# Sorting the first expert layer's tokens for half of the batches

## The chip, the cores and the metric

The kernel runs on one core of a Trainium2 chip, as one launch. The metric is the device time of that launch in microseconds (us). TensorE (PE), VectorE (DVE), ScalarE (ACT), GpSimd (POOL) and the DMA queue of SyncE (SP) run their own programs and meet through semaphores.

## What is computed

Two layers over x, 4 batches of 512 tokens with 256 features. Cut to what matters:

```python
# layer 0, for each batch b
w_bot = einsum('g,got->ot', cond_8[b], weight * mask)      # a projection mixed from 8
h = x @ w_bot.T + bias
probs = softmax(h @ router_w.T);  top 2 of 8 experts, weights topk_w
x = x + sum over the 2 chosen experts e of topk_w[e] * (h @ W0[e] + probs[e])    # W0[e]: 256x256
# layer 1, for each batch b
h = x @ W_base.T + b_base + lora(cond_8[b])
shared = 2 experts for all tokens: (silu(h @ wg) * (h @ wu)) @ wd                # hidden width 352
routed = the same form, for the top 2 of 8 other experts of each token
x = x + shared + routed
```

All products are made of f16 halves: a value is split in a high and a low part, and three products (high by high, low by high, high by low) are summed.

## The kernel before

A **tile** is 128 tokens; there are 16, four to a batch. Three stages follow each other.

**Dense layer 0** (main PE loop over `m` in `range(TWO)`, TWO = 8, two tiles a step). For each of the 16 tiles TensorE multiplies by all 8 experts: for each pair of experts `j` 6 matmuls of 512 columns into one PSUM bank (`group`, L1000). VectorE adds `coef * result` to `x1` for every expert, chosen or not (L777, 8 a tile; `coef` is 0 for the six not chosen). Four banks turn, so TensorE is at most two pairs ahead of VectorE. Laid between: `transposes(m)` turns the finished tiles of `x1`, ScalarE and VectorE split them (`tr_hi`, `tr_lo`), `layer1_input(c)` projects batch c for layer 1, `h_hi`/`h_lo` split the result, `logits(1, c)` gives its gate values, `token_rows` and `copy_rows` turn it into rows of tokens, which SP stores in HBM (`keep`, `token_store`).

At the same time the 21,760 columns of layer 1 weights are loaded and split in 16 **pieces** of 1,360 columns, through two buffers. SP may load piece n when piece n-2 is through (`s_pclo` at n-1 or more). ScalarE makes the high half and scales the piece (`split_piece`, L529 and L532), GpSimd subtracts in eight parts (L442) to give the low half. ScalarE takes two pieces in each step m, at places fixed in its program.

**Shared steps.** The shared experts' work is 24 steps, six to a batch (`ST`). A step is `gate_up(i)` on TensorE (12 matmuls of 512 columns, the sixth of a batch 6), a silu on ScalarE (L572), a product on VectorE (`prod`, L904), a copy to f16 on ScalarE (`acts`, L582) and a subtraction on VectorE (L910). After six, `down(c)` (68 matmuls of 256 columns) and four `accumulate` follow. The first EARLY = 18 steps run before the routed loop. Among them the chosen experts of all 2,048 tokens become slots of a sorted list: `largest`, `second` (13 small VectorE instructions), `ranks` on TensorE, `groups`, `slots`, `hot_lanes`, `hot_tiles`, `inverse` on TensorE, `slot_tokens`, `tile_experts`, one of them after each of steps 2 to 14.

**Routed loop and end.** 39 tiles of 128 slots, each of one expert. GpSimd fetches rows by index (L451) and puts results by index (L456). After it SP loads the results, ScalarE scales them, GpSimd adds one (L470), VectorE the other (`combine`, L892), beside the last six shared steps.

## Time and profile before

| | us |
|---|---|
| median of 3 runs (lowest, highest) | 379.43 (377.74, 380.24) |
| the profiled execution, its own time | 378.77 |
| its span, first to last instruction | 377.0 |
| TensorE busy in the span | 357.7 |
| VectorE, ScalarE, GpSimd busy | 238.8, 166.1, 154.2 |
| mean granted TensorE clock | 0.994 of full |

The page gives for each engine the busy time, for each line of code a group of instructions with its mean length, and the idle time before it with the instruction that ended the idle time. The timeline gives the same in order of time. A program of this kind has no scheduler: each engine does its own list in the written order, and an instruction that waits holds up all that stands behind it on its engine.

### The profile page before, as it was taken

How to read it: one execution, taken by the hardware profiler on the slowest of the kernel's cores; microseconds unless marked ns; L12 is line 12 of the kernel's file. 1: busy time of each engine (PE TensorE's matmuls, PEld its weight loads, DVE VectorE, ACT ScalarE, POOL GpSimd, SP SyncE). 2: the span in 40 equal slices, each digit the busy share in tenths (PEclk: the TensorE clock that was granted, in tenths of full speed). 3: DMA queues.
4: the chain of work that ended last, by engine and by line, in shares of the span. 5: the costliest groups of instructions: out<-in, count | busy, mean ns of one | idle time of the engine just before them, and what ended most of it. 6: DMA issues, size and time to landing. Idle time of an engine off the chain costs nothing.

```text
span 377.0 us, 7974 instructions
## 1 busy us (share of the span) xinstructions
PE 357.7 (95%) x2713; PEld 225.4 (60%) x2714; DVE 238.8 (63%) x594; ACT 166.1 (44%) x286; POOL 154.2 (41%) x241
## 2 busy tenths in 40 slices
PE   7998999999999999989999999999999999999992
PEld 3543544455454454555447677777777777776561
DVE  1357999676766646778775455565555565546476
ACT  1045376567555765543442333333333333323560
POOL 3000564665647532000020365565665555532642
PEclk9999999999999999999999999999999999999997
DMA  7985113433443420100000122222222222212942
GB/s 217 377 330 203 54 53 119 150 92 122 141 151 128 136 69 0 58 0 2 0 28 2 44 86 84 70 84 78 75 83 80 73 78 78 80 42 74 353 161 111
DMA packets 18038, 39.26 MB, mean 104 GB/s; under 512 B 2976, under 2 KB 9376, under 8 KB 17888
## 3 DMA queue, kind: packets, MB, share of 16 engines
q1 hardware_dynamic: 13552, 28.71, 22.8%
q0 software_dynamic: 3744, 10.23, 8.7%
q8 instruction: 14, 0.23, 0.3%
q10 hardware_dynamic: 720, 0.02, 0.1%
q14 instruction: 8, 0.07, 0.1%
HBM read 29.65 MB, written 9.31 MB: 103 GB/s over the span
## 4 chain that ended last, share of the span: by engine, by line
PE 72%; DVE 16%; DMA 4%; ACT 3%; issue 3%; SPq 0%; DVEq 0%
PE bank L1000 58%; PE bank L1147 4%; PE bank L1245 3%; DVE prod L904 2%; PE bank L1016 2%; PE bank L1229 2%; ACT acts L582 2%; DVE x L892 2%; DMA w1s<-results 2%; DVE x L777 2%; DVE acts L910 1%; DMA x<-wc 1%; PE bank L1076 1%; DMA results<-yb,row_out 1%; ACT sil L572 1%
## 5 line engine op out<-in xcount | busy, mean ns | idle before, releaser
L442 POOL TENSOR_TENSOR w1s<-piece,w1s 128x170 f16<-128x170 f32 x128 | 61.6, 521 | 78.2 <-ACT piece L532 78.2
L1000 PE MATMUL bank<-w0s,hs 128*128 128x512 f16 x384 | 86.0, 379 | 1.2 <-DVE x L777 1.2
L1000 PE MATMUL bank<-w1s,rT 128*128 x468 | 76.2, 313 | 1.6 <-DVE rT L964 1.6
L451 POOL DMA_INDIRECT rows<-token_store,row_in x39 | 37.9, 971 | 86.1 <-DVE row_in L874 47.5
L777 DVE SCALAR_TENSOR_TENSOR x<-bank,coef,x 128x256 f32<-128x256 f32 x128 | 54.8, 478 | 19.4 <-PE bank L1000 19.1
L1000 PEld LDWEIGHTS bank<-w0s,hs 128*128 128x128 f16 x384 | 36.9, 98 | 43.8 <-DVE x L777 1.9
L1000 PE MATMUL bank<-hs,w1s 128*128 128x512 f16 x264 | 59.6, 379 | 2.1 <-DVE prod L904 2.1
L1000 PEld LDWEIGHTS bank<-w1s,rT 128*128 128x128 f16 x468 | 44.0, 98 | 22.1 <-issue 2.1
L456 POOL DMA_INDIRECT results<-yb,row_out x39 | 38.5, 987 | 37.1 <-ACT yb L606 37.1
L1000 PE MATMUL bank<-w1s,aT 128*128 (+1 forms) x351 | 44.8, 273 | 0.8 <-DVE aT L957 0.8
L600 ACT ACTIVATE ract<-prod 128x352 f16<-128x352 f32 x39 | 19.4, 497 | 58.5 <-DVE prod L970 33.6
L1000 PEld LDWEIGHTS bank<-hs,w1s 128*128 128x128 f16 x264 | 25.0, 98 | 32.3 <-DVE prod L904 5.2
L964 DVE COPY rT<-bank 128x256 f32<-128x256 f32 x39 | 16.6, 425 | 33.3 <-PE bank L1229 33.3
L1000 PEld LDWEIGHTS bank<-w1s,aT 128*128 128x128 f16 (+1 forms) x351 | 32.7, 98 | 4.5 <-issue 0.9
L973 DVE TENSOR_TENSOR ract<-prod,ract 128x352 f16<-128x352 f32 x39 | 20.5, 526 | 21.9 <-issue 18.5
L1147 PE MATMUL bank<-w1s,acts 128*128 128x256 f16 x272 | 30.5, 273 | 1.5 <-DVE slot_lo L839 1.2
L595 ACT ACTIVATE sil<-bank 128x352 f32<-128x352 f32 x39 | 18.1, 463 | 28.5 <-PE bank L1000 28.5
L1147 PEld LDWEIGHTS bank<-w1s,acts 128*128 128x128 f16 x272 | 26.4, 98 | 6.1 <-issue 1.7
L582 ACT ACTIVATE acts<-prod 128x512 f16<-128x512 f32 (+1 forms) x24 | 15.1, 629 | 30.7 <-DVE prod L904 30.7
L529 ACT ACTIVATE w1s<-piece 128x1360 f16<-128x1360 f32 x16 | 21.3, 1329 | 14.7 <-DMA piece<-w 14.7
L910 DVE TENSOR_TENSOR acts<-prod,acts 128x512 f16<-128x512 f32 (+1 forms) x24 | 16.7, 697 | 16.0 <-ACT acts L582 16.0
L532 ACT ACTIVATE piece<-piece 128x1360 f32<-128x1360 f32 x16 | 21.4, 1338 | 0.5
(149 smaller groups left out, 405.5 us busy)
## 6 DMA issues: line engine op xcount, KB each, us to landing
piece<-w SPq DMA_DIRECT2D x16, 680.0 KB, 3.9
w1s<-results SPq DMA_DIRECT2D x6, 512.0 KB, 8.3
x<-wc SPq DMA_DIRECT2D x4, 512.0 KB, 7.0
w1s<-xT SPq DMA_DIRECT2D x4, 512.0 KB, 11.0
w1s<-w SPq DMA_DIRECT2D x4, 512.0 KB, 10.1
token_store<-xrow SPq DMA_DIRECT2D x4, 512.0 KB, 3.3
out<-x SPq DMA_DIRECT2D x8, 256.0 KB, 2.2
x<-x SPq DMA_DIRECT2D x1, 1536.0 KB, 11.7
```

What stands on the lines that cost most here:

```text
L442: ins = nc.gpsimd.tensor_tensor(w1s[:, LO, at], piece[:, i % 2, part], w1s[:, HI, at], ALU.subtract)
L451: pool.indirect_dma_start(rows[:, i % 2], None, token_store, bass.IndirectOffsetOnAxis(row_in[:, i:i + 1], 0)).then_inc(s_row[i % 2], 16)
L456: pool.indirect_dma_start(results, bass.IndirectOffsetOnAxis(row_out[:, i:i + 1], 0), yb[:, i % 2], None).then_inc(s_put[i % 2], 16)
L529: nc.scalar.activation(w1s[:, HI, i * PIECE:(i + 1) * PIECE], piece[:, i % 2], ACT.Copy, scale=SW).then_inc(sm["s_pchi"], 1)
L532: nc.scalar.activation(piece[:, i % 2], piece[:, i % 2], ACT.Copy, scale=SW).then_inc(sm["s_pcsc"], 1)
L582: nc.scalar.activation(acts[0:M, c % 2, f, HI], prod[0:M, p], ACT.Copy).then_inc(sm["s_ahi"], 1)
L600: nc.scalar.activation(ract[:, q, HI], prod[:, q, 0:F], ACT.Copy).then_inc(sm["s_rhi"], 1)
L777: nc.vector.scalar_tensor_tensor(x1[:, t], bank[(n + a) % 4][:, h * D:(h + 1) * D], coef[:, t, e:e + 1], x1[:, t], ALU.mult, ALU.add).then ...
L910: nc.vector.tensor_tensor(low, prod[0:M, p], acts[0:M, c % 2, f, HI], ALU.subtract).then_inc(sm["s_alo"], 1)
L973: nc.vector.tensor_tensor(ract[:, q, LO], prod[:, q, 0:F], ract[:, q, HI], ALU.subtract).then_inc(sm["s_rlo"], 1)
L1000: mm = nc.tensor.matmul(out_ap, l, r, start=(i == 0), stop=(i == len(terms) - 1))
L1147: mm = nc.tensor.matmul(bank[4 + q][:, 0:D], acts[:, c % 2, f, a, q * P:(q + 1) * P], w_dn(b, f), start=(f == 0 and n == 0), stop=(f == ST ...
```

## The change

Batches 0 and 1 (tiles 0 to 7) keep the dense layer 0. Batches 2 and 3 (tiles 8 to 15) get a sorted one: TensorE turns their layer 0 input into rows (`rows_of_layer0`), VectorE works out a slot for each of the 2,048 choices (`slots0`), GpSimd scatters the rows into `slot_rows` in HBM (16 indirect DMAs), SP loads 23 tiles of slots, TensorE turns each (`operand_rows`) and multiplies it by one expert (`sorted_tile`, 6 matmuls of 256 columns), SP stores the results in `slot_out`, GpSimd gathers them (16 indirect DMAs) and VectorE adds them with their weights (`combine0`, four instructions for two tiles). The sorted tiles run in bursts of four behind the shared steps 2 to 7. The dense loop has 4 steps m instead of 8. EARLY is 21 instead of 18; the dense stage's work for batches 2 and 3 and `down(0)`, `down(1)` stand behind step 11, the ranks and slots of layer 1 behind steps 12 to 19. Pieces are taken in the order 0 to 9, 13, 14, 15, 10, 11, 12, and pieces from the ninth on are split among the shared steps, since the first layer's weights and buffers now lie where they go.

The core of the diff:

```diff
-    EARLY = 3 * ST
-    DOWN = {ST + 1: 0, EARLY - 1: 1, EARLY + 1: 2}
+    EARLY = 3 * ST + 3
+    DOWN = {EARLY + 1: 2}
...
+    TILES0 = (NTR * P * K_TOP + E * (P - 1)) // P
+    BURST = 4
+    BURST_AT = 2
+    DEEP = 4
...
+    ORDER = [*range(FREE), *range(KEPT, NP), *range(FREE, KEPT)]
...
+            for n in range(FREE - 2):
+                load_piece(n)
...
+            keep(0)
+            sp.wait_ge(sm["s_placed"], 16 * K_TOP * NTR)
+            for i in range(DEEP):
+                load_rows0(i)
+            load_piece(FREE - 2)
+            for i in range(TILES0):
+                if i + DEEP < TILES0:
+                    load_rows0(i + DEEP)
+                keep_out0(i)
+                if i == BURST:
+                    load_piece(FREE - 1)
...
+            for n in range(4):
+                low_parts(n)
+            pool.wait_ge(sm["s_slots0"], 1)
+            pool.wait_ge(sm["s_zero"], 16 * 2)
+            for t in range(NTR):
+                for k in range(K_TOP):
+                    place(t, k)
+            for n in range(4, FREE):
+                low_parts(n)
+            for b in range(DEEP):
+                pool.wait_ge(s_kept0[b], 16 * len(range(b, TILES0, DEEP)))
+            for t in range(TPB):
+                take(t)
+            low_parts(FREE)
+            for t in range(TPB, NTR):
+                take(t)
...
+                if m == 1:
+                    copy_rows0(range(NTD, NTD + TPB))
...
+                if i == 10:
+                    exps(2, DENSE, 1.0 / (SH1 * SW))
+                if i == 11:
+                    tr_hi(4)
+                    piece_hi(FREE + 2)
+                    tr_hi(5)
+                    piece_scaled(FREE + 2)
+                    h_hi(1, 2)
+                    tr_hi(6)
+                    tr_hi(7)
+                    h_hi(1, 3)
...
+                if i == 11:
+                    transposes(4)
+                    down(0, quarters=(0, 1))
+                    transposes(5)
+                    down(0, quarters=(2, 3))
+                    layer1_input(2)
+                    transposes(6)
+                    down(1, quarters=(0, 1))
+                    transposes(7)
+                    down(1, quarters=(2, 3))
+                    layer1_input(3)
```

**GpSimd.** From the first subtraction on, before:

```order
L442 TENSOR_TENSOR w1s<-piece,w1s 128x170 x128
L451 DMA rows<-token_store,row_in 128x512 x6
L456 DMA results<-yb,row_out 4352x256
```

and now:

```order
L545 TENSOR_TENSOR w1s<-piece,w1s 128x170 x32
L555 DMA slot_rows<-xrow,idx 2944x512 x16
L545 TENSOR_TENSOR w1s<-piece,w1s 128x170 x48
L560 DMA yg<-slot_out,idx 128x256 x8
L545 TENSOR_TENSOR w1s<-piece,w1s 128x170 x8
L560 DMA w1s<-slot_out,idx 128x256 x8
L545 TENSOR_TENSOR w1s<-piece,w1s 128x170 x40
L590 DMA rows<-token_store,row_in 128x512 x6
```

The subtractions of the fifth piece now stand behind 16 scatters, which wait for the slot numbers (`s_slots0`).

**ScalarE** in step m = 3 of the dense loop, with the rows of the change (the rows before are the same up to their line numbers, with two additions of the bias instead of four): the halves of layer 1's input (L618), the seventh piece (L672, L677), the turned tiles (L658), the LoRA weights, the bias, the token rows (L663), the eighth piece.

```order
L618 ACTIVATE hs<-bank,b_sc 128x512 [waits s_h,s_bsc]
L618 ACTIVATE hs<-bank,b_sc 128x512 [waits s_h]
L672 ACTIVATE w1s<-piece 128x1360 [waits s_piece6]
L677 ACTIVATE piece<-piece 128x1360 [waits s_pchi]
L658 ACTIVATE xrow<-bank 128x2x256 [waits s_tr]
L697 ACTIVATE wls<-wl 128x512 [waits s_wlf]
L654 ACTIVATE x<-x,st 128x256 x4
L663 ACTIVATE xrow<-bank 128x512 [waits s_rt] x4
L672 ACTIVATE w1s<-piece 128x1360 [waits s_piece7]
L677 ACTIVATE piece<-piece 128x1360 [waits s_pchi]
```

The order is kept; what the wait for `s_piece6` hangs on has moved.

**ScalarE** from shared step 10 to the first turned tiles of batch 2, now (no such stretch before):

```order
L738 ACTIVATE sil<-bank 128x512 [waits s_prod,s_gu]
L750 ACTIVATE acts<-prod 128x512 [waits s_prod]
L672 ACTIVATE w1s<-piece 128x1360 [waits s_m0,s_piece11]
L640 ACT_TABLE_LOAD
L640 ACTIVATE ex<-ex 128x64 [waits s_exq]
L738 ACT_TABLE_LOAD [waits s_prod]
L738 ACTIVATE sil<-bank 64x512 [waits s_gu]
L750 ACTIVATE acts<-prod 64x512 [waits s_prod]
L677 ACTIVATE piece<-piece 128x1360 [waits s_pchi]
L658 ACTIVATE xrow<-bank 128x2x256 [waits s_tr]
```

The exponentials of the first two batches, with their two table loads, stand between steps 10 and 11.

## Rows read from the trace of the kernel before

**Rows 1.** The page, part 1: busy us, share of span, instructions.

```profile
PE 357.7 (95%) x2713; PEld 225.4 (60%) x2714; DVE 238.8 (63%) x594; ACT 166.1 (44%) x286; POOL 154.2 (41%) x241
```

**Rows 2.** Windows: stretch, its length, busy us of each engine, granted clock, DMA.

```profile
136.66:206.62 69.96, 65.97 (x461) 38.01 (x458) 47.76 (x130) 32.57 (x51) 5.88 (x10) 1.00 0.06 20
85.30:136.66 51.36, 51.36 (x316) 25.97 (x314) 33.46 (x75) 32.12 (x39) 30.12 (x64) 1.00 0.39 123
```

**Rows 3.** Timeline of TensorE: start us, us, line, what.

```profile
81.21 0.61 PE L1087 MATMUL bank<-ident,hs 128*128 128x128 f16 x8
81.66 2.75 PE L1000 MATMUL bank<-w0s,hs 128*128 128x512 f16 x12
...
85.30 5.34 PE L1000 MATMUL bank<-w0s,hs 128*128 128x512 f16 x24
```

**Rows 4.** Groups by line and shape: count, busy us, mean ns, idle before.

```profile
L1000 PE MATMUL bank<-w0s,hs 128*128 128x512 f16 x384 | 86.0, 379 | 1.2 <-DVE x L777 1.2
L442 POOL TENSOR_TENSOR w1s<-piece,w1s 128x170 f16<-128x170 f32 x128 | 61.6, 521 | 78.2 <-ACT piece L532 78.2
L1147 PE MATMUL bank<-w1s,acts 128*128 128x256 f16 x272 | 30.5, 273 | 1.5 <-DVE slot_lo L839 1.2 <-DVE acts L910 0.3
L532 ACT ACTIVATE piece<-piece 128x1360 f32<-128x1360 f32 x16 | 21.4, 1338 | 0.5
L964 DVE COPY rT<-bank 128x256 f32<-128x256 f32 x39 | 16.6, 425 | 33.3 <-PE bank L1229 33.3
L524 ACT ACTIVATE xrow<-bank 128x512 f16<-128x512 f16 x16 | 8.7, 595 | 11.0 <-PE bank L1087 11.0
```

**Rows 5.** Timeline of VectorE in the dense stage.

```profile
46.64 0.25 DVE L721 COPY lg<-bank 128x96 f32<-128x96 f32 x1
...
50.59 3.23 DVE L777 SCALAR_TENSOR_TENSOR x<-bank,coef,x 128x256 f32<-128x256 f32 x8
...
65.31 0.68 DVE L749 SCALAR_TENSOR_TENSOR wl<-wb_in,bank 128x512 f32<-128x512 f32 x1
```

**Rows 6.** Timeline of GpSimd: its two indirect DMAs with no wait between.

```profile
191.63 1.16 POOL L451 DMA_INDIRECT rows<-token_store,row_in  x1 [47.48 <-DVE row_in L874]
193.10 0.95 POOL L451 DMA_INDIRECT rows<-token_store,row_in  x1 [0.30 <-issue]
```

**Rows 7.** The page, part 6: DMA issues, KB each, us to landing.

```profile
piece<-w SPq DMA_DIRECT2D x16, 680.0 KB, 3.9
out<-x SPq DMA_DIRECT2D x8, 256.0 KB, 2.2
```

**Rows 8.** Timeline of VectorE among the shared steps.

```profile
168.79 1.39 DVE L848 TENSOR_SCALAR yg<-lane,slot_lo 128x128 f16<-128x128 f16 x8
...
175.76 0.69 DVE L904 SCALAR_TENSOR_TENSOR prod<-bank,sil 128x512 f32<-128x512 f32 x1 [0.35 <-ACT sil L572]
177.15 0.69 DVE L910 TENSOR_TENSOR acts<-prod,acts 128x512 f16<-128x512 f32 x1 [0.70 <-ACT acts L582]
177.76 1.45 DVE L854 TENSOR_TENSOR wls<-tile,slot_hi 128x1248 f16<-128x1248 f16 x1
```

**Rows 9.** Timeline of ScalarE: a table load before the exponentials.

```profile
168.17 1.28 ACT L501 ACT_TABLE_LOAD   x1
```

**Rows 10.** Timeline of VectorE: the first routed tile, and the end.

```profile
206.62 0.41 DVE L964 COPY rT<-bank 128x256 f32<-128x256 f32 x1
...
367.16 5.02 DVE L892 SCALAR_TENSOR_TENSOR x<-w1s,st,x 128x256 f32<-128x256 f32 x8
372.21 1.42 DVE L922 SCALAR_TENSOR_TENSOR x<-bank,x 128x256 f32<-128x256 f32 x4
```

**Rows 11.** Windows of 1 us at the end, columns as in Rows 2.

```profile
369.00:370.00 1.00, 0.54 (x5) 0.23 (x3) 1.00 (x2) 0.00 (x0) 1.00 (x2) 1.00 0.22 86
...
372.00:373.00 1.00, 0.00 (x0) 0.00 (x0) 0.97 (x4) 0.00 (x0) 0.00 (x0) 0.62 0.21 76
373.00:374.00 1.00, 0.00 (x0) 0.00 (x0) 0.63 (x2) 0.00 (x0) 0.00 (x0) 0.50 0.18 70
```

More of the change, by code:

```diff
@@ L899, in shared_dve @@
                 up = bank[2 * p + 1][0:M] if f < ST - 1 else bank[2 * p][0:M]
+                last = len(turned_rows(i)) - 2
+                first = max(last - 2, 0)
+                for t in turned_rows(i)[:first]:
+                    operand0(t)
                 dve.wait_ge(sm["s_sil"], i + 1)
@@ L906, in shared_dve @@
                 if i == 1:
-                    h_lo(1, B - 1)
+                    h_lo(1, 1)
+                for t in turned_rows(i)[first:last]:
+                    operand0(t)
                 dve.wait_ge(sm["s_ahi"], i + 1)
@@ L928, in _ @@
+            tr_lo(TWO_D - 1)
             for i in range(EARLY):
                 shared_dve(i)
[L930 to L940 removed]
@@ L941, in _ @@
-                if i == 12:
+                if i == 9:
+                    dve.wait_ge(sm["s_m0"], TILES0)
+                    take_logits(1, 0, DENSE)
+                    largest(DENSE)
+                    second(DENSE)
+                    selected(DENSE, "s_sel")
+                if i == 11:
+                    combine0(8)
+                    tr_lo(4)
+                    accumulate(0, (), (0, 1))
+                    combine0(10)
+                    tr_lo(5)
+                    accumulate(0, (), (2, 3))
+                    h_lo(1, 2)
+                    combine0(12)
+                    tr_lo(6)
+                    accumulate(1, (), (0, 1))
+                    combine0(14)
+                    tr_lo(7)
+                    accumulate(1, (), (2, 3))
+                    h_lo(1, 3)
@@ new lines, in _ @@
+                if i == 12:
+                    take_logits(1, 1, SORTED)
+                    largest(SORTED)
+                    second(SORTED)
+                    selected(SORTED, "s_sel")
+                if i == 14:
+                    dve.wait_ge(sm["s_rank"], 1)
+                    groups(rank1[:, NT * E:])
+                    slots()
+                if i in (15, 16):
+                    hot_lanes(2 * (i - 15))
+                    hot_lanes(2 * (i - 15) + 1)
+                if i == 17:
+                    for n in range(3):
+                        hot_tiles(n)
@@ new lines, in sorted_tile, with experts0 @@
+            def sorted_tile(i, expert_at):
+                pe.wait_ge(sm["s_x0"], i + 1)
+                if i >= 2:
+                    pe.wait_ge(sm["s_y0"], i - 1)
+                group(bank[6 + i % 2][:, D:2 * D],
+                      [(rT0[:, i % 2, a, k], w1s[:, b, bass.ds(expert_at + (W0 + k * E * D), D)])
+                       for k in range(KT) for a, b in PASSES], "s_m0")
+            def experts0(ap):
+                return nc.values_load_multi_w_load_instructions(
+                    ap, engines=(nc.tensor.engine,), min_val=0, max_val=(E - 1) * D,
+                    skip_runtime_bounds_check_because="the table's entries are clamped where it is made")[1]
```

548 lines of the change are left out of this document (380 added, 168 removed).

## The prediction

> **What bounds the kernel now.** I read the page's busy times first: TensorE is busy 357.7 of 377.0 us [rows 1]. Then the windows of the two stretches that the change rebuilds: in 85.30 to 136.66 (steps m = 4 to 7 of the dense loop) it is busy all of 51.36 us, in 136.66 to 206.62 (from `gate_up(0)` to the first routed tile) 65.97 of 69.96 [rows 2]. So TensorE sets the pace and 12.1 us of saved TensorE work (below) could be a gain. But VectorE is busy 47.8 of the second stretch's 70 us, and its timeline shows why that is nearly all it can do: of each shared step it works 0.69, waits 0.70 for ScalarE's copy, and works 0.69 [rows 8]. The slack is thin, and every engine runs a fixed list.
>
> **TensorE's work before the routed loop.** Removed: 8 tiles x 24 dense matmuls = 192, at 86.0 / 384 = 0.224 us: 43.0 [rows 4]. Added: 23 sorted tiles x 6 = 138 matmuls of 256 columns at 30.5 / 272 = 0.112: 15.5; 92 + 32 transposes, 8 in the 0.45 between two starts: 0.056 each, 7.0 [rows 3]; the small ranks 0.6; three shared steps that come forward from behind the loop 7.8 (12 matmuls each). Net -12.1. The rest is moved. From here the question is who is late. I follow the written order with row durations; times are on the clock of the trace before.
>
> **Step 1, to `gate_up(0)`.** Until m = 1 nothing changes but a cast: VectorE begins m = 1 at 50.8 instead of 50.59 [rows 5]. In m = 1 TensorE stands before the rows of tile 10 until ScalarE has copied tile 8, which ScalarE does behind `tr_hi(0)` and `wl_hi(1)`: 56.2 instead of 51.9. The rows of tiles 14 and 15 wait once more, behind the bias, which needs `shares0`. VectorE is 4.0 late at m = 2. The ranks on TensorE hold it again, `groups` cost 1.4 and `slots0` 1.3, so that it passes the point where it stood at 65.31 [rows 5] at 74.8, and the slot numbers are there.
>
> GpSimd then issues 16 scatters. The only pair without a wait gives 0.95 + 0.30 = 1.25 a scatter [rows 6]; the busy part alone, 0.95, is the lower bound, the pair's start to start, 1.47, the upper. I take 1.27 with a little for the wait each carries: 20.3, ending at 95.1. Behind them the fifth piece's subtraction takes 8 x 61.6 / 128 = 3.85 [rows 4]. Only then may SP load the seventh piece, which needs its buffer: 3.9 to landing [rows 7]. It is there at 102.9, where ScalarE has waited since 84.7. Behind the wait stand its two passes of 1.34 each [rows 4], the turned tiles, LoRA weights, four additions of the bias, and the four copies of token rows for which TensorE stands since 93.3. It resumes at 108.9, and `gate_up(0)` starts at **109.5** instead of 136.66: -27.2. Without the scatters in the way it would be 93.9. The hold of 15.6 is the largest single wait.
>
> **Step 2, `gate_up(0)` to the end of the sorted tiles.** Steps 0 and 1, `layer1_input(1)` and step 2 reach the burst after 11 us. A burst is 4 x (0.67 + 0.22) = 3.6 of TensorE work with 2.6 of gate_up. VectorE (four copies of 0.425 [rows 4], 2.1 for the step) and ScalarE (four copies, a silu, a copy, one pass of a piece: 4.0) fit. What does not quite fit is the load of the last tile of a burst: SP may issue it only when the first result of the burst is stored, and a load takes about 2.2 [rows 7]: 0.5 a burst. The tenth piece's load stands in the same queue: 2.0 once. Sum 48.7 for 43.9 of work. `gate_up(0)` + 48.7 is S.
>
> **Step 3, steps 8 to 11.** TensorE has 10.0 of work. GpSimd gathers once the last result is stored (S + 3.2); the first four gathers land by S + 10.3. They are not the last to come: ScalarE has in steps 8 to 11 four pairs of silu and copy, four token rows (8.7 / 16 = 0.54 each [rows 4]), four passes of a piece (5.4), and the exponentials with two table loads of 1.28 [rows 9]; VectorE puts 15 small instructions of batches 0 and 1 in between (3.3, by 3.95 for the 96-column form, 46.64 to 50.59 [rows 5]). Followed in order: step 11's subtraction ends at S + 20.8, four `combine0` of 0.63 [rows 10] at S + 23.3. TensorE idles 13.4.
>
> **Step 4, the block behind step 11.** TensorE 22.2: 136 matmuls x 0.112, 4 transposes of tiles, two `layer1_input`. Three times it then waits for VectorE's accumulate and the next combine0: 2.9 + 3.9 + 2.9. Ends S + 54.7.
>
> **Step 5, steps 12 to 20.** TensorE 27.7. VectorE has the other batches' top two (3.3), `groups` and `slots` (3.8), 32 hot lanes (1.39 for 8 [rows 8]: 5.6), `hot_tiles` 3.5, `slot_tokens` 1.6 and `tile_experts` 1.8 beside nine steps of 2.1; before they had steps 2 to 14 to lie in, now 12 to 19. ScalarE has 4.4 a step in steps 12 to 15 and again two table loads. In order: hot tiles ready at S + 90.9, row numbers at S + 94.4, expert numbers at S + 99.1, `gate_up(20)` ends S + 102.6; the first routed copy follows step 20's subtraction at S + 105.3. That is `gate_up(0)` + 154.0 where before it was 69.96 [rows 2]: **+84.0**. The first routed copy is at 263.5 instead of 206.62 [rows 10].
>
> **Step 6, the end.** The routed loop is the same. Behind it three shared steps are gone: VectorE lost 2.1 to each between combines, up to 372.21 [rows 10]. Its other work stays, and GpSimd's 16 additions cap what it gains: **-5.5**.
>
> **The clock.** [...] How long it stays there no row of the trace shows: the lower bound is 0; for the upper I let down's first two quarters (3.8) and `gate_up(0)` and half of (1) (3.9) take double. I take the middle, 1.9 each: **+3.8**. [...]
>
> **Sum.** 378.77 (the profiled execution, span 377.0) - 27.2 + 84.0 - 5.5 + 3.8 = 433.9. The median of the three runs is 0.7 above that execution, within their spread of 2.5. **Forecast 434.**
>
> **Rivals.**
> - *TensorE stays the bound* (faster). If no engine is ever later than TensorE, the gain is 12.1 + 5.5: 361. For it: rows 1. Against it: it needs all the waits above (some 65 us) to vanish; it decides from the point where the seventh piece is there before TensorE is through m = 3, at 93.3 by my chain, 9.6 before it can be. 3%.
> - *Only the scatters' hold counts*: from `gate_up(0)` on, TensorE's 103.8 of work runs without waits: 378.77 - 27.2 + 33.8 - 5.5 = 380. The change does not do what it should, nor harm. 4%.
> - *Half of the late waits*: order costs less than I chain, steps 3 to 5 overlap in part: about 405. 13%.
> - *GpSimd's indirect DMAs cost more back to back* than the one pair shows, 2.5 us each as their 128 KB are written: +20 on step 1 and something on step 3, 456. 9%.
> - *The clock stays low* in the sparse stretch from S: 50 us of TensorE work, half of it on the path, doubled: +25, 459. 8%.
> - Forecast, its own range 421 to 443 (scatters 15.2 to 23.5 in all, step 2 45 to 50, clock 0 to 7.7): 63%.
>
> The range for 8 in 10 is 402 to 450. Within 1% counts as no change. Faster 3%, same 3%, slower 94%.
>
> **What would show it.** Right: 16 scatters in a row on GpSimd that end near 95 and an idle time of ScalarE before the seventh piece of about 18 us, ended by its load; `gate_up(0)` near 109; TensorE idle before the turning of tile 8, ended by combine0; VectorE over 90% busy in steps 14 to 18; the first routed tile near 263. Wrong: scatters under 0.8 us, or a first routed tile before 235, which would mean that the orders of steps 8 to 20 overlap better than written.

## The result and the profile after

| | before | after |
|---|---|---|
| median (lowest to highest), us | 379.36 (377.74 to 380.24), 4 runs | 460.21 (459.58 to 462.46), 4 runs |
| the profiled execution, its span | 378.77, 377.0 | 462.46, 460.7 |
| mean granted TensorE clock | 0.994 | 0.901 |

The change is slower, with a ratio of 1.2148 (95% interval 1.2089 to 1.2207). The forecast was 434 and the range 402 to 450: the direction and most of the mechanism held, the size did not. Some 26 us more were lost than I had summed.

The page, part 1, after, which answers to [rows 1]: busy us, share of the span, instructions.

```profile
PE 363.9 (79%) x2799; PEld 234.7 (51%) x2800; DVE 244.4 (53%) x605; ACT 181.2 (39%) x320; POOL 190.3 (41%) x274
```

Over the whole span TensorE has some 20 us less to multiply (the prediction's 12.1 ahead of the loop, and the 7.8 of the three steps that only moved), but is busy for 6 us more than before. So it took some 26 us longer for its work (an estimate: 363.9 against 357.7 less 19.9): part of it ran at a lower granted clock, 0.901 of full in the mean against 0.994. Windows of the changed kernel: stretch, its length, busy us of PE, weight load, DVE, ACT, POOL, then the granted clock, DMA share and GB/s.

```profile
60.00:75.00 15.00, 12.34 (x70) 5.89 (x69) 9.01 (x27) 8.08 (x10) 2.59 (x6) 0.81 0.10 42
100.00:120.00 20.00, 5.74 (x22) 3.13 (x23) 4.40 (x11) 11.05 (x16) 13.32 (x28) 0.50 0.40 126
185.00:200.00 15.00, 0.23 (x1) 0.23 (x2) 9.12 (x14) 7.12 (x8) 12.55 (x17) 0.62 0.53 175
200.00:215.00 15.00, 12.90 (x77) 9.98 (x77) 4.24 (x9) 3.64 (x4) 7.14 (x16) 0.70 0.20 62
260.00:275.00 15.00, 8.68 (x48) 4.15 (x49) 12.16 (x31) 6.51 (x9) 7.85 (x11) 0.62 0.00 1
```

Before, the clock was 1.00 in the stretches of [rows 2]. Now it is 0.50 to 0.81 in these stretches, in which TensorE has stood, and still low when the work starts again: 0.50 in 114 to 120, 0.58 in 199 to 207, 0.50 in 261.7 to 267.

GpSimd, after, timeline (start us, us, line, what, and in brackets the idle time before and what ended it): the first and the last of the sixteen scatters, and the fifth and sixth pieces' subtractions behind them.

```profile
80.18 1.17 POOL L555 DMA_INDIRECT slot_rows<-xrow,idx  x1 [3.99 <-DVE idx L999]
...
99.76 0.96 POOL L555 DMA_INDIRECT slot_rows<-xrow,idx  x1 [0.30 <-issue]
100.74 7.46 POOL L545 TENSOR_TENSOR w1s<-piece,w1s 128x170 f16<-128x170 f32 x16
```

ScalarE, after: the seventh piece's first pass.

```profile
108.42 1.34 ACT L672 ACTIVATE w1s<-piece 128x1360 f16<-128x1360 f32 x1 [18.84 <-DMA piece<-w]
```

The sixteen take 20.6 us, 1.285 each: the pair of [rows 6] had the right price. ScalarE stands 18.84 us before the seventh piece, as forecast (about 18). TensorE, after, timeline: the same hold as it sees it, then the later waits and the work behind them.

```profile
56.54 1.01 PE L1375 MATMUL bank<-ident,hs 128*128 128x128 f16 x8 [4.37 <-ACT xrow L686]
57.35 5.21 PE L1284 MATMUL bank<-w1s,hs 128*128 128x512 f16 x12
...
114.26 1.09 PE L1400 MATMUL bank<-ident,hs 128*128 128x128 f16 x8 [16.16 <-ACT xrow L663]
115.14 2.77 PE L1284 MATMUL bank<-hs,w1s 128*128 128x512 f16 x6
...
144.13 0.55 PE L1501 MATMUL bank<-ident,w1s 128*128 128x128 f16 x4 [3.03 <-DMA w1s<-slot_rows]
144.53 4.27 PE L1284 MATMUL bank<-hs,w1s 128*128 128x512 f16 x12
...
166.47 2.75 PE L1284 MATMUL bank<-hs,w1s 128*128 128x512 f16 x12 [0.56 <-issue]
...
199.77 1.12 PE L1363 MATMUL bank<-ident,x 128*128 128x128 f32 x4 [16.54 <-DVE x L1035]
200.68 6.32 PE L1468 MATMUL bank<-w1s,acts 128*128 128x256 f16 x34
...
220.83 0.66 PE L1363 MATMUL bank<-ident,x 128*128 128x128 f32 x4 [3.14 <-DVE x L1035]
...
261.77 5.30 PE L1284 MATMUL bank<-hs,w1s 128*128 128x512 f16 x12 [5.59 <-DVE prod L1113]
271.62 2.26 PE L1524 MATMUL bank<-wls,yg 128*128 128x78 f16 x32 [4.55 <-DVE wls L1064]
...
283.42 4.80 PE L1284 MATMUL bank<-hs,w1s 128*128 128x512 f16 x12 [5.17 <-DVE te L1090]
291.43 3.41 PE L1284 MATMUL bank<-w1s,rT 128*128 x12 [2.99 <-DVE rT L1248]
```

Twelve matmuls of 512 columns take 2.75 us at the full clock (at 166.47) and 5.2 to 5.3 here behind a wait of 4.4 or 5.6 (granted 0.56 in 57 to 63, 0.50 in 261.7 to 267); a routed tile's first twelve take 3.41 where before they took 1.96. The stretches against my forecast:

| from to | forecast, us | measured, us | miss |
|---|---|---|---|
| start to `gate_up(0)` | 109.5 | 115.1 | +5.6 |
| to `gate_up(8)` (S) | 48.7 | 58.0 | +9.3 |
| to the turning of tile 8 | 23.3 | 26.7 | +3.4 |
| to `gate_up(12)` | 31.4 | 34.3 | +2.9 |
| to the first routed tile's products (50.6 to its copy, 0.6 on) | 51.2 | 57.3 | +6.1 |
| to the last instruction (169.8 before, less 5.5) | 164.3 | 169.3 | +5.0 |
| clock, a term of its own | 3.8 | in the rows above | -3.8 |

Together +28.5, and the span is 28.6 longer than 377.0 + 55.1. This execution is the slowest of its four; the median stands 2.3 us under it. With the same code up to there, `gate_up(0)` starts at 113.2 to 114.9 in the profiles of experiments 4, 6, 8, 10 and 11, and the row "to `gate_up(12)`" takes 31.3 to 32.2 in experiments 4, 8, 10 and 11. So a difference of 2 or 3 us between two profiles is no effect by itself.

### The profile page after: what moved, and what is told of

The parts are those of the page before. It is cut to its first block, busy times and chain, and to the rows that moved or that the text cites. A ratio compares the mean times of both kernels' runs of the same rounds, so it can differ in the third digit from the quotient of the medians.

```text
span 460.7 us, 8449 instructions
## 1 busy us (share of the span) xinstructions
PE 363.9 (79%) x2799; PEld 234.7 (51%) x2800; DVE 244.4 (53%) x605; ACT 181.2 (39%) x320; POOL 190.3 (41%) x274
## 4 chain that ended last, share of the span: by engine, by line
PE 55%; DVE 17%; DMA 9%; ACT 8%; issue 5%; POOL 4%; SPq 1%; DVEq 0%; ACTq 0%
PE bank L1284 42%; PE bank L1468 4%; POOL slot_rows L555 3%; DMA w1s<-slot_rows 3%; PE bank L1608 3%; PE bank L1592 2%; DVE x L1097 2%; DMA piece<-w 2%; DVE prod L1113 2%; DMA w1s<-results 2%; DVE x L1035 1%; DMA x<-wc 1%; ACT acts L750 1%; DVE x L1156 1%; PE bank L1300 1%
## 5 line engine op out<-in xcount | busy, mean ns | idle before, releaser
L545 POOL TENSOR_TENSOR w1s<-piece,w1s 128x170 f16<-128x170 f32 x128 | 64.9, 543 | 147.7 <-ACT piece L677 147.7
L1284 PE MATMUL bank<-w1s,rT 128*128 x606 | 96.6, 307 | 6.2 <-DVE rT L1248 3.9
L1284 PE MATMUL bank<-hs,w1s 128*128 128x512 f16 x264 | 70.9, 425 | 13.8 <-DVE prod L1113 7.5
L1284 PEld LDWEIGHTS bank<-w1s,rT 128*128 128x128 f16 x606 | 56.8, 99 | 31.2 <-issue 7.8
L1284 PE MATMUL bank<-w1s,hs 128*128 128x512 f16 x192 | 49.2, 416 | 0.0
L1113 DVE SCALAR_TENSOR_TENSOR prod<-bank,sil 128x512 f32<-128x512 f32 (+1 forms) x24 | 16.5, 688 | 42.1 <-ACT sil L738 42.0
L1468 PE MATMUL bank<-w1s,acts 128*128 128x256 f16 x272 | 34.3, 292 | 0.0
L1156 DVE SCALAR_TENSOR_TENSOR x<-bank,coef,x 128x256 f32<-128x256 f32 x64 | 26.7, 474 | 13.0 <-PE bank L1284 12.9
L1284 PEld LDWEIGHTS bank<-w1s,hs 128*128 128x128 f16 x192 | 19.7, 105 | 24.7 <-issue 7.2
L1468 PEld LDWEIGHTS bank<-w1s,acts 128*128 128x128 f16 x272 | 28.6, 105 | 5.3
L672 ACT ACTIVATE w1s<-piece 128x1360 f16<-128x1360 f32 x16 | 21.3, 1329 | 23.9 <-DMA piece<-w 23.9
L790 ACT ACTIVATE sil<-bank 128x352 f32<-128x352 f32 x39 | 18.1, 463 | 25.1 <-PE bank L1284 25.1
L738 ACT ACTIVATE sil<-bank 128x512 f32<-128x512 f32 (+1 forms) x24 | 14.3, 595 | 34.0 <-PE bank L1284 33.8
## 6 DMA issues: line engine op xcount, KB each, us to landing
w_raw<-w SPq DMA_DIRECT2D x4, 512.0 KB, 11.1
```

Source lines behind the costliest of these rows:

```text
L545: ins = nc.gpsimd.tensor_tensor(w1s[:, LO, at], piece[:, n % 2, part], w1s[:, HI, at], ALU.subtract)
L672: nc.scalar.activation(w1s[:, HI, ORDER[n] * PIECE:(ORDER[n] + 1) * PIECE], piece[:, n % 2], ACT.Copy, scale=SW).then_inc(sm["s_pchi"], 1)
L790: nc.scalar.activation(sil[:, q, 0:F], bank[2 * q][:, 0:F], ACT.Silu, scale=1.0 / (SH1 * SW)).then_inc(sm["s_rsil"], 1)
L1113: nc.vector.scalar_tensor_tensor(prod[0:M, p], up, SA / (SH1 * SW), sil[0:M, p], ALU.mult, ALU.mult).then_inc(sm["s_prod"], 1)
L1156: nc.vector.scalar_tensor_tensor(x1[:, t], bank[(n + a) % 4][:, h * D:(h + 1) * D], coef[:, t, e:e + 1], x1[:, t], ALU.mult, ALU.add).then ...
L1284: mm = nc.tensor.matmul(out_ap, l, r, start=(i == 0), stop=(i == len(terms) - 1))
```

## The experiments

The times are medians of four runs (twelve in the fifth), against 460.21 for the change and some 379.5 for the kernel before.

**1. Subtractions among the scatters.**

```diff
-            for n in range(4):
+            for n in range(5):
                 low_parts(n)
...
             for t in range(NTR):
+                if t == 4:
+                    low_parts(5)
                 for k in range(K_TOP):
                     place(t, k)
-            for n in range(4, FREE):
+            for n in range(6, FREE):
```

> The change, but GpSimd subtracts the fifth piece ahead of the sixteen scatters and the sixth after eight of them. Theory (the scatters hold the seventh piece, and through it ScalarE's list and TensorE): the fifth piece was scaled at 76.1, so its 3.8 end at 80, when the slot numbers come; the seventh piece lands near 84, ScalarE's idle time of 18.8 before it goes, gate_up(0) starts near 99 instead of 115.1, the whole is about 16 us shorter: 444. Rival 1 (something else would hold TensorE there, for instance the loads of the sorted tiles behind the last scatter at 104.4): under 5 us of it remain. Rival 2 (scatters are slow for their writes, and slow the subtractions beside them): subtractions over 5 us a piece, scatters over 1.5 each, gain under 8.

447.55 us, ratio 1.1762 (1.1721 to 1.1803): 12.7 less than the change. The hold is gone, and something new stands in its place. GpSimd, experiment 1:

```profile
91.82 3.78 POOL L545 TENSOR_TENSOR w1s<-piece,w1s 128x170 f16<-128x170 f32 x8
...
105.72 7.92 POOL L545 TENSOR_TENSOR w1s<-piece,w1s 128x170 f16<-128x170 f32 x16
```

VectorE, experiment 1:

```profile
106.46 6.83 DVE L1123 TENSOR_TENSOR acts<-prod,acts 128x512 f16<-128x512 f32 x1 [0.70 <-ACT acts L752]
```

TensorE, experiment 1:

```profile
98.99 1.46 PE L1286 MATMUL bank<-hs,w1s 128*128 128x512 f16 x6
115.27 0.81 PE L1286 MATMUL bank<-rs,hs 128*128 128x8 f16 x24 [5.31 <-DVE hs L832]
```

`gate_up(0)` starts at 98.99 (expected near 99). But VectorE's subtraction of 0.69 us [rows 8] lasts 6.83: it began behind the start of a row of sixteen subtractions on GpSimd and ended 0.35 before that row did. TensorE waits 5.31 for what stands behind it. From `gate_up(0)` to these 24 small matmuls it is 16.3 us instead of 13.4, so 2.9 of the 16.2 gained went there; against the 10.8 that this stretch takes in experiment 2, at the full clock and without the hold by GpSimd, it is 5.5. Neither theory had it.

**2. Unused matmuls (spins) in the two long waits.**

```diff
+            def spin(n, b, col):
+                for _ in range(n):
+                    nc.tensor.matmul(bank[b][:, D - 192:D], ident16[:], hs[:, HI, 0, col:col + 192],
+                                     start=True, stop=True)
...
                             logits(1, 0)
+                            spin(170, 7, 3 * S)
                             token_rows(0, (2, 3))
...
                 if i == 11:
+                    pe.wait_ge(sm["s_x0"], TILES0)
+                    pe.wait_ge(sm["s_rows"], ND * TPB)
+                    spin(170, 5, 0)
                     transposes(4)
```

> The change, with 170 unused matmuls of 192 columns (some 14 us) on TensorE in each of its two longest waits (16.2 us before the token rows of tiles 2 and 3, 16.5 before the turning of tile 8); their results are read by nothing. It prices the clock alone. [...] Rival (what is slow is VectorE's and ScalarE's chain, and TensorE at half clock is hidden beside it): the granted clock is full in 100 to 120 and 186 to 215, but the time moves by under 2 us. If the matmuls outlast the waits, their excess shows as lost time, at most 2 us a wait.

456.43 us, ratio 1.2041 (1.1996 to 1.2086): 3.8 less, about half of the 6 to 8 that I had expected for the theory that the slow restarts lie on the path. TensorE, experiment 2:

```profile
177.87 14.19 PE L1420 MATMUL bank<-hs,ident 128*128 128x192 f16 x170
194.07 0.66 PE L1363 MATMUL bank<-ident,x 128*128 128x128 f32 x4 [2.01 <-DVE x L1035]
194.56 3.88 PE L1474 MATMUL bank<-w1s,acts 128*128 128x256 f16 x34
```

The 34 matmuls take 3.88 instead of 6.32, with the clock granted at 1.00 in 194 to 199, where the change has 0.58 in 199 to 207: the low clock was what made them slow. From `gate_up(0)` to `gate_up(8)` the profile shows 55.0 instead of 58.0, and the turnings of tiles 8 and 10 are 6.5 apart instead of 9.3. (This execution is the fastest of its four, 452.80 of up to 459.01.) Part is given back later, where the clock falls in a wait of 3.15 that left it high in the change: the third turning takes 1.12 instead of 0.66, the 34 matmuls behind it 4.94 instead of 3.88 (granted 0.74 in 210.6 to 216.5, against 1.00 in 220.8 to 225.3 of the change).

**3. Three shared steps more ahead of the loop, in the kernel before.**

```diff
-    EARLY = 3 * ST
-    DOWN = {ST + 1: 0, EARLY - 1: 1, EARLY + 1: 2}
+    EARLY = 3 * ST + 3
+    DOWN = {ST + 1: 0, 3 * ST - 1: 1, EARLY + 1: 2}
```

(and the scaling and the bank side placed as in the change)

> The kernel before, with 21 shared steps ahead of the routed loop instead of 18, and nothing else. My prediction's terms for it: 7.8 us of gate_up more ahead of the loop, 5.5 less behind it: +2.3 us, 382. Theory now (behind the loop the end hangs on the loads of the results and GpSimd's additions, and loses nothing when three steps leave): +7 us, 386 to 387, with the stretch from the loop's end to the last instruction as long as before within 1 us.

386.18 us, ratio 1.0147 (1.0108 to 1.0185): the total is the theory's, its reason is not. TensorE, experiment 3, the first routed tile:

```profile
218.21 3.70 PE L1000 MATMUL bank<-w1s,rT 128*128 x12 [2.99 <-DVE rT L964]
```

It starts 11.0 later than the 207.17 of before, not 7.8: with no `down` behind the last shared step, TensorE stands 2.99 for the first copy and then needs 3.70 for what took 1.96. The end does get shorter. The last store of a routed tile, GpSimd, experiment 3, and the same one after the change:

```profile
356.25 0.97 POOL L456 DMA_INDIRECT results<-yb,row_out  x1 [1.38 <-ACT yb L606]
```

```profile
428.37 0.97 POOL L595 DMA_INDIRECT results<-yb,row_out  x1 [1.32 <-ACT yb L801]
```

From there to the end of the span it is 28.7 here, 32.3 after the change, and 34.3 before (342.68 to 377.0). So my 5.5 for the tail was right (5.6). What hid it in the change is the closing: SP's waits at the end, first after the change, then in experiment 3 (line, what it waited for, us in total, times, longest).

```profile
SPq L106 <- PEq L106: 4.5, 1, 4.5
```

```profile
SPq L85 <- PEq L85: 1.1, 1, 1.1
```

Behind the last landing the change waits 3.4 us longer for TensorE's sequencer.

**4. The tenth piece's load ahead of the sorted tiles.**

```diff
             load_piece(FREE - 2)
+            load_piece(FREE - 1)
             for i in range(TILES0):
...
                 keep_out0(i)
-                if i == BURST:
-                    load_piece(FREE - 1)
```

> The change, with the tenth piece's load issued ahead of the loads and stores of the sorted tiles instead of after the fifth. Theory (TensorE's wait of 3.0 us at 144 for the rows of a sorted tile is for a load that stands behind the 680 KB of that piece, and the clock falls after it): the wait goes, the next 12 matmuls take 2.8 instead of 4.3, 3 to 5 us shorter, 456. Rival (the wait is of the store or load chain itself, four deep): nothing moves, 460. Rival 2: the piece collides with the rows of tiles 4 to 7 instead, and the wait moves to 133: 459 to 460.

454.28 us. Its four runs, 448.33, 452.61, 455.95 and 458.10, lie too far apart for an interval: the total says only that it is shorter, by 2 to 12 us. The size comes from the profile: from `gate_up(0)` to `gate_up(8)` it is 53.1 instead of 58.0. TensorE, experiment 4, where the wait of 3.03 and the slow twelve stood:

```profile
138.82 0.40 PE L1500 MATMUL bank<-ident,w1s 128*128 128x128 f16 x4
139.22 2.75 PE L1283 MATMUL bank<-hs,w1s 128*128 128x512 f16 x12
```

No wait, and 2.75 instead of 4.27 (granted 1.00 in 139 to 142, against 0.65 in 144.5 to 149 of the change). One load in a queue cost 3.0 us of wait and here 1.5 of clock (in experiment 2, after 2.83 in the same place, the twelve took 2.75).

**5. Twenty-nine semaphores more, in the kernel before.**

```diff
+        spare_sems = [sem(f"s_spare{c}") for c in range(29)]
```

> The kernel before with 29 more semaphores declared, as many as the change declares, and used by nothing. In the change SP's last wait, for TensorE's sequencer behind the last store, is 4.5 us; in the kernel before with 21 early steps it is 1.1. Theory (the semaphores are set back at the end, one after another): +3 to 3.5 us, 383. Rival (the closing hangs on the program's length or on the sorted stage's registers): no change, 379.6.

379.39 us, ratio 0.9998 (0.9975 to 1.0022), SP's last wait 1.1 as before. The theory falls, for semaphores that nothing uses. Every kernel built on the change shows 3.7 to 4.5 there, both built on the kernel before 1.1. The cause stays open.

**6. One top two, exponentials behind step 20.**

```diff
                 if i == 9:
                     dve.wait_ge(sm["s_m0"], TILES0)
                     take_logits(1, 0, DENSE)
-                    largest(DENSE)
-                    second(DENSE)
-                    selected(DENSE, "s_sel")
...
                     take_logits(1, 1, SORTED)
-                    largest(SORTED)
-                    second(SORTED)
-                    selected(SORTED, "s_sel")
+                    largest(ALL)
+                    second(ALL)
+                    selected(ALL, "s_sel")
...
-                if i == 10:
-                    exps(2, DENSE, 1.0 / (SH1 * SW))
-                if i == 15:
-                    exps(3, SORTED, 1.0 / (SH1 * SW))
+            exps(2, ALL, 1.0 / (SH1 * SW))
```

> The change, with the top two of all sixteen tiles of layer 1 worked out once, behind step 12, instead of twice (behind steps 9 and 12), and its exponentials once, behind step 20, instead of behind steps 10 and 15 between the silus. VectorE has 3.3 us and a wait of 3.4 beside GpSimd's subtraction less before tile 8 is turned, ScalarE two table loads there (2.6) and two in step 15. Theory (VectorE's and ScalarE's lists hold TensorE in steps 8 to 11 and 12 to 20): the turning of tile 8 comes 3 to 6 us sooner, the first routed tile 5 to 8 sooner, 453. Rival (the gathers hold it: their last for tiles 8 and 9 lands near 188, and GpSimd's list is unchanged): under 2 us. Rival 2: VectorE's list behind step 12 only gets longer by the wider forms: 459 to 460.

459.19 us, ratio 1.2088 (1.2028 to 1.2148): within 1% of the change. TensorE and VectorE, experiment 6:

```profile
191.73 1.11 PE L1357 MATMUL bank<-ident,x 128*128 128x128 f32 x4 [11.14 <-DVE x L1032]
202.69 0.66 PE L1357 MATMUL bank<-ident,x 128*128 128x128 f32 x4 [4.28 <-DVE x L1032]
...
214.46 1.11 PE L1357 MATMUL bank<-ident,x 128*128 128x128 f32 x4 [3.15 <-DVE x L1032]
215.36 6.33 PE L1462 MATMUL bank<-w1s,acts 128*128 128x256 f16 x34
```

```profile
199.51 3.12 DVE L1032 SCALAR_TENSOR_TENSOR x<-yg,part,x 128x256 f32<-128x256 f32 x4
```

The wait before tile 8 falls from 16.5 to 11.1, so the first theory was right there. Then combine0 meets GpSimd's next subtraction (3.12 for four instead of 1.66) and the wait before tile 10 rises from 2.1 to 4.3; the turnings of tiles 8 to 14 span 32.1 instead of 27.5. The larger part of that loss is the clock and not VectorE: it fell in the wait of 3.15 before tile 12 (0.59 in 214.4 to 221.7), though the change kept it high through the 3.14 at 220.83 (1.00 in 220.8 to 225.3), and the 34 matmuls behind tiles 12 and 14 take 6.33 and 5.11 instead of 3.88 each. What was saved ahead was lost behind, and a good part of it by a clock that differs between executions; the total of 459 to 460 that rival 2 named has another reason than the one it gave, since from `gate_up(12)` to the first routed tile it is 57.0, no longer than the 57.3 of the change.

**7. All of these at once, and all gathers ahead of the eleventh piece.** The edits of 1, 4 and 6, a third subtraction among the scatters (`if t == 6: low_parts(6)`), and

```diff
-            for t in range(TPB):
-                take(t)
-            low_parts(FREE)
-            for t in range(TPB, NTR):
+            for t in range(NTR):
                 take(t)
```

> Everything together that removes a wait from the change: subtractions of the fifth to seventh piece among the scatters, the tenth piece's load before the sorted tiles, one top two and one set of exponentials, all gathers ahead of the eleventh piece's subtraction. Theory (the losses are separate places of one chain): the gains add, 12.7 + 5.9 + about 7, and the 6.8 us that VectorE's subtraction waited beside GpSimd's run of sixteen in the first experiment come on top: 425 to 432. Rival (one wait replaces another): over 440. Neither expects it under the kernel before.

444.18 us, ratio 1.1695 (1.1638 to 1.1751): the rival. TensorE, experiment 7:

```profile
120.48 0.61 PE L1495 MATMUL bank<-ident,w1s 128*128 128x128 f16 x4 [5.01 <-DMA w1s<-slot_rows]
```

ScalarE, experiment 7:

```profile
173.33 1.34 ACT L672 ACTIVATE w1s<-piece 128x1360 f16<-128x1360 f32 x1 [3.67 <-DMA piece<-w]
...
189.03 1.34 ACT L672 ACTIVATE w1s<-piece 128x1360 f16<-128x1360 f32 x1 [8.15 <-DMA piece<-w]
```

The ninth and tenth pieces, 680 KB each, are now issued together at 111.6 just ahead of the rows of the fifth sorted tile, and that tile waits 5.01. With the gathers first, the pieces behind them come late, and ScalarE stands 3.67 and 8.15 us for them. These two cost TensorE nothing that the rows show: tile 8 is turned 21.0 us behind `gate_up(8)` (21.3 in experiment 6), tile 10 waits 4.28 in both, and its copy on ScalarE comes 0.03 after the turning. The block behind step 11 is long, 40.5 us to `gate_up(12)` as in experiment 6 (34.3 in the change), since its four groups of 34 matmuls run slow: 5.74, 5.54, 6.32 and 5.10.

**8. Unused matmuls in the four late waits** (50 before `gate_up(18)`, 40 before `inverse`, 45 before `gate_up(20)`, 25 before the first routed tile).

> The change, with unused matmuls of 192 columns on TensorE in the four waits before the routed tiles: 50 before gate_up(18), 40 before inverse, 45 before gate_up(20), 25 before the first routed tile (4.1, 3.3, 3.7 and 2.1 us). It prices the clock in 255 to 295. Theory (TensorE's bursts of 5.30, 2.26, 4.57, 4.80 and 3.41 us at about half clock lie on the path between VectorE's parts): 5 to 9 us shorter, 453. Rival (VectorE's list is what takes the time, TensorE only answers to it): the groups take 2.8, 1.4, 2.8, 2.8 and 2.0 us, but the first routed tile comes under 2 us sooner.

454.84 us, ratio 1.2003 (1.1952 to 1.2054): 5.4 less. TensorE, experiment 8:

```profile
256.48 2.76 PE L1284 MATMUL bank<-hs,w1s 128*128 128x512 f16 x12 [1.13 <-DVE prod L1113]
...
268.39 4.68 PE L1284 MATMUL bank<-hs,w1s 128*128 128x512 f16 x12
...
284.21 1.96 PE L1284 MATMUL bank<-w1s,rT 128*128 x12 [0.93 <-DVE rT L1248]
```

From `gate_up(17)` (249.41; 254.71 in the change) to the first routed tile it is 34.8 instead of 36.7, and that tile's twelve are 1.4 shorter: the profile gives 3.4 to the spins, between the two theories; the first routed tile alone, 1.9 sooner, fits the rival. The rest of the 5.4 lies ahead of them, where this execution restarted faster than the profiled one of the change (the turnings of tiles 8 and 10 are 8.0 apart instead of 9.3) with the same code. The spin before `inverse` was too short: 3.79 us of wait are left behind it and the next twelve still take 4.68.

**9. Mended with the collisions avoided, and spins.** Of experiment 7 without the change of the gathers, the ninth piece's load moved ahead of the wait for the scatters and the tenth's behind the first four sorted tiles' rows, with the spins of experiment 8 and 110 before tile 8.

```diff
+            load_piece(FREE - 2)
             sp.wait_ge(sm["s_placed"], 16 * K_TOP * NTR)
             for i in range(DEEP):
                 load_rows0(i)
-            load_piece(FREE - 2)
+            load_piece(FREE - 1)
```

> The subtractions of pieces five to seven among the scatters, the ninth piece's load ahead of the wait for the scatters and the tenth's behind the rows of the first four sorted tiles, one top two and one set of exponentials, the gathers in the order of the change, and unused matmuls in the waits before tile 8 (110 of 192 columns) and in the four waits before the routed tiles. Theory (the change's loss is a sum of replaceable waits and of slow restarts): what the seventh experiment lost to two pieces that met the rows of the sorted tiles (5.0 and a slow burst) and to the late twelfth piece (8.2) comes back, and the clock gives 5 more: 426 to 432. Rival (what is mended here opens the next wait): 438 or more. Both stay above the kernel before.

430.11 us, ratio 1.1344 (1.1295 to 1.1393): the theory's time, 30.1 us below the change. TensorE, experiment 9, the first sorted tile's rows, and before tile 8:

```profile
112.65 1.02 PE L1503 MATMUL bank<-ident,w1s 128*128 128x128 f16 x8 [2.63 <-DMA w1s<-slot_rows]
...
163.78 7.84 PE L1417 MATMUL bank<-hs,ident 128*128 128x192 f16 x93
173.25 0.65 PE L1360 MATMUL bank<-ident,x 128*128 128x128 f32 x4 [1.64 <-DVE x L1035]
173.74 3.87 PE L1470 MATMUL bank<-w1s,acts 128*128 128x256 f16 x34
```

The first line of the spins is where the view begins; all 110 take 9.24 from 162.38. Against experiment 7 the profile is 19.0 shorter, in two places mainly: 54.0 instead of 60.4 from `gate_up(0)` to `gate_up(8)`, where the collision went, and 29.8 instead of 40.5 from the turning of tile 8 to `gate_up(12)`, where all four groups of 34 take 3.87 or 3.88 (7.2 less) and tile 10 waits 2.10 instead of 4.28. So the clock gave more than the 5 expected, and the late twelfth piece not the 8.2. After the wait of 2.63 above the clock was low too, 0.59 in 112.65 to 115.1: eight transposes took 1.02 instead of 0.61.

**10. The expert taken as number 0 for all sorted tiles** (`places0 = [0] * BURST`), so TensorE loads no register in a burst. The kernel leaves out the choice of the first layer's expert.

> The change with the first layer's expert taken as number 0 for all 23 sorted tiles instead of read from the table, so that TensorE loads no register in a burst (its result is left out of the computation; matmuls, loads and stores are the same). Theory (six groups of register loads stall TensorE 0.4 to 0.6 us each behind steps 2 to 7, not in my sum): 2 to 3 us shorter there, 457.5. Rival (TensorE has slack for them beside the loads of the rows): under 1 us. SP's last wait of 4.5 us: if it hangs on these loads it falls to 1.1.

457.03 us, ratio 1.2067 (1.2007 to 1.2127): 3.2 less, but its interval overlaps that of the change, and by the profile only 0.6 of it comes from where the loads stood. TensorE, experiment 10:

```profile
143.34 0.61 PE L1501 MATMUL bank<-ident,w1s 128*128 128x128 f16 x4 [4.28 <-DMA w1s<-slot_rows]
```

From `gate_up(0)` to `gate_up(8)` it is 57.4 instead of 58.0. In the changed kernel a burst can end with a wait like the 0.56 at 166.47 that nothing but "issue" ends. Three of these, 1.1 us in all, stand in its waits between 120 and 173, and none here; in four bursts the shared step's matmuls follow the turned rows 0.24 later instead of 0.39 to 0.96, 1.8 in all. So the loads cost 1 to 2 us. What they gave, the tenth piece took back: the wait is 4.28 instead of 3.03, and the twelve behind it take 5.33 instead of 4.27. The rest of the 3.2 lies in code that is the same in both. SP's last wait is 3.7, so it doesn't hang on them.

**11. Eighteen early steps in the change.**

```diff
-    EARLY = 3 * ST + 3
+    EARLY = 3 * ST
```

(and the hot tiles, `inverse`, `slot_tokens` and `tile_experts` behind step 17)

> The change with 18 shared steps ahead of the routed loop instead of 21; the hot tiles, the slot's tokens and the tile's experts all stand behind step 17. In the kernel before, three steps more ahead cost 6.6 us: 11.0 on the first routed tile, 5 given back behind it. Theory (in the change VectorE's slot work fills steps 12 to 20, so TensorE's 7.8 us for the three steps lie partly in its waits): the first routed tile comes 5 to 8 us sooner, the end takes 5 more, 457 to 460. Rival (they lie wholly on the path): 454. Rival 2 (they hide entirely): 465.

451.87 us, ratio 1.1925 (1.1856 to 1.1994): 8.3 less, beyond even the rival's. TensorE, experiment 11:

```profile
267.63 2.26 PE L1522 MATMUL bank<-wls,yg 128*128 128x78 f16 x32 [15.44 <-DVE wls L1064]
```

The first routed tile comes at 276.5, 14.9 sooner than in the change, and the end costs 4.2 more (36.5 from the last store). `inverse` itself is only 4.0 sooner. But from `inverse` to the routed tile it is 8.9 instead of 19.8. By these rows the three steps had not lain in VectorE's shadow: each had put a product, a wait for ScalarE and a subtraction between two parts of VectorE's slot work.

**12. Experiment 9 with eighteen early steps** (spins of 135 before and 50 behind `inverse`).

> The ninth experiment with 18 shared steps ahead of the routed loop instead of 21, the slot work behind step 17 as in the eleventh, and unused matmuls in the two waits that this leaves (135 of 192 columns before inverse, 50 behind it). Theory (both gains are of separate places): the 8.3 us of the eleventh less the 3 to 4 that the spins of the ninth gave in steps 18 to 20: 424 to 427. Rival (VectorE's slot work, all in one place now, takes the gain back): 429 or more. Neither comes under the kernel before.

431.93 us, ratio 1.1385 (1.1347 to 1.1424): the rival's time, but not for its reason. ScalarE, experiment 12, the copy of tile 8, which TensorE had turned at 174.8:

```profile
179.11 0.60 ACT L661 ACTIVATE xrow<-bank 128x512 f16<-128x512 f32 x1 [6.23 <-remote]
```

It comes 4.3 us after its input was there, and no row says what it waited for ("remote" is a release that the profile cannot name). Behind it combine0 meets GpSimd's subtraction (2.70 for four), tile 10's turning waits 5.81 (2.10 in experiment 9) and its 34 matmuls take 4.95. So the block behind step 11 takes 36.2 instead of 29.8, in code that is the same in both. From `gate_up(12)` to the first routed tile it is 46.1 instead of 55.4, 9.3 gained (10.9 in experiment 11), and from there to the end 5.2 longer. The gain of the moved slot work was there; what took it back lies ahead of it, and its cause is open. The first routed tile comes at 256.4, only 2.0 sooner than in experiment 9. No version I built comes under the kernel before; the best is 50.7 us above it.

## Why the prediction was too low

**Right.** TensorE's own work fell, and the waits took much more than that. Step 1's mechanism is as written, only 5.4 us later: slot numbers, sixteen scatters at 1.285 (taken 1.27), the subtraction, the seventh piece, ScalarE idle for 18.8; experiment 1 removes it for 16.2 us at `gate_up(0)` (forecast 15.6). Step 6's 5.5 is confirmed by experiment 3. Combine0 at 0.63 was too much: four take 1.66. The rivals "TensorE stays the bound", "only the scatters' hold counts" and "half of the late waits" are out, and so is "the indirect DMAs cost more": they cost what [rows 6] showed.

**The clock, mis-sized: the step that failed.** I charged 3.8, for the work behind two long waits at half the full clock, and left out the short waits. No row of before shows how long the clock stays low when work begins again; [rows 11] show only that it was at 0.62 and then 0.50 behind TensorE's last matmul. So the 3.8 was an estimate that no run shows. In its place, the rows of the profiled execution give some 18 us on TensorE's path (an estimate, from these rows and the same stretches in other runs), and all of TensorE's work took 26 longer. By stretch, in us:

| | miss | low clock | other causes | left |
|---|---|---|---|---|
| to `gate_up(0)` | 5.6 | 4.2, the twelves at 57.35 and 68.87 | | 1.4 |
| to `gate_up(8)` | 9.3 | 2.6 behind `gate_up(0)`, 1.5 at 144.53 | tenth piece's wait 1.0 above my 2.0, register loads 1.8, small waits for rows and copies 0.7 above my 2.8 | 1.7 |
| to tile 8 | 3.4 | | VectorE held by GpSimd 3.1 | 0.3 |
| to `gate_up(12)` | 2.9 | 4.5, against experiment 9 | | -1.6 |
| to the first routed tile | 6.1 | 3.9, `gate_up(19)` and `gate_up(20)` | | 2.2 |
| to the end | 5.0 | 1.4, the first routed tile | closing 3.4 | 0.2 |

The clock's 18.1 less my 3.8 are 14 of the 28.5, the other causes 10, and 4 are open. What runs bear this out: experiment 2 took off 3.8 (two waits, 1.5 given back), experiment 8 3.4 by its profile, and in experiment 9 the block behind step 11 is 4.5 shorter than in the change. For m = 1 there is no run, but executions of the same code differ: in experiment 4 the two twelves took 3.84 and 3.79 instead of 5.21 and 4.44, 2.0 less, and from the rows of tile 10 to `gate_up(0)` it was 57.0 instead of 58.6. `gate_up(19)` and `gate_up(20)` are on the path by their silus: ScalarE's idle times before these, 5.46 and 7.98, end by TensorE. Of the two experiment 8 mended the second alone, and the stretch was 1.9 shorter.

Behind short waits the work was slow too: after waits of 4.4 us at 56.5 and 5.6 at 261.8 twelve matmuls take 5.2 and 5.3 instead of 2.75. But the three waits of step 4 did not lose the clock by themselves here: they were 2.10, 3.14 and 2.10, and behind the last two 34 matmuls took 3.88. In experiments 1, 2, 6 and 7 the same 3.14 to 3.15 was followed by 5.11, 4.94, 6.33 and 6.32.

**Step 2, 48.7 for 58.0.** I put the tenth piece at 2.0: it was 3.0 of wait and 1.5 of clock, and moving its load made the stretch 4.9 shorter (experiment 4). I had no term for the register loads at all: 1 to 2 by experiment 10.

**Steps 3 to 5.** In order and kind as written, but VectorE and GpSimd hold each other up, which I had no row for. VectorE, after:

```profile
186.15 3.37 DVE L894 TENSOR_TENSOR t<-oh 128x64 f32<-128x64 f32 x1
```

GpSimd, after:

```profile
186.16 3.75 POOL L545 TENSOR_TENSOR w1s<-piece,w1s 128x170 f16<-128x170 f32 x8
...
268.26 6.50 POOL L545 TENSOR_TENSOR w1s<-piece,w1s 128x170 f16<-128x170 f32 x8 [6.91 <-ACT piece L677]
```

An instruction of 0.22 us lasts 3.37, and ends 0.4 before GpSimd's run. It cost 3.1 in step 3; without it, in experiment 6, the stretch is 5.4 shorter, with the two table loads gone as well. Step 4's forecast was 1.6 too long for the full clock (29.8 in experiment 9), which hid a part of what the clock cost there. VectorE was busy 84% of the time from step 14's product (247.2) to the end of the hot tiles (271.6), not the over 90% that I named as a sign.

**Step 6.** The term was right; the closing's 3.4 and the slow first routed tile's 1.4 ate it. Neither was in my sum.

**The rival "the clock stays low" (459, 8%)** comes nearest to the measured time, by a sum that did not happen: behind `gate_up(8)` the clock came back after each wait (twelve matmuls in 2.75 from 214.9 to 254.7, the routed loop from 295.7 on at its old 1.96), and what it cost there is some 10 us by the table, not 25.

**The range** was built on the size of known terms and took no room for unknown ones. The upper bound of the clock term, 7.7, covered two waits; the clock was low in nine places. Costs that I had no row for (register loads 1 to 2, the engines' mutual wait 3.1, the closing 3.4) make another 8 us.

## What to carry to other kernels

When TensorE, busy 95% of the time as here, gets idle gaps, charge every gap twice: once as a wait and once for the slow work behind it. In the profiles of this case gaps of 4.4 us and more were always followed by slow work (twelve matmuls in 5.2 to 5.3 instead of 2.75 in the change), gaps of 2.6 to 3.2 in some executions and not in others. Follow the written order of each queue, since one 680 KB load or one run of subtractions in the wrong place cost 3 to 16 us; and expect that taking one wait away opens another, so that gains measured alone do not add. Work moved "into a shadow" lengthens the list of the engine that casts it.
